# Copying the last 50 expert tiles' weights inside SBUF, gathering the third group without landing waits, two merged VectorE products, and new instruction orders

## What is computed

```python
x = x + ga * L0_attn(norm(x))            # RWKV: time mix, k, v, r, wkv scan, output, channel mix
x = x + gb * L0_ffn(norm(x))             # 128 -> 512 -> 128
x = x + ga1 * L1_attn(norm(x))           # softmax attention
h = norm(x); logits = h @ W_router + b_router
top_vals, top_idx = top_k(logits, 2)
for e in range(8):
    y = relu(h @ W1[e] + b1[e]) @ W2[e] + b2[e]      # 128 -> 512 -> 128
    out += y * softmax_weight[:, e]                  # 0 where e is not among the token's two
x = x + gb1 * out
```

## Time and profile before

| | before |
|---|---|
| median of 3 runs | 1623.48 us |
| lowest, highest | 1614.8, 1625.54 us |
| span of the profiled execution | 1622.0 us |
| PE busy | 1353.9 us (83%) |
| DVE busy | 1095.2 us (68%) |
| ACT busy | 990.8 us (61%) |
| POOL busy | 545.8 us (34%) |
| moved by DMA | 217.68 MB |
| loads of expert weights (mW, inner, wide) | 109 + 31 + 16, 514 KB each |

### The profile page before, as it was taken

One profiled execution on the slowest core, in us unless ns is written; L12 is line 12 of the kernel. 1 busy time (PEld: TensorE's weight loads), 2 busy tenths in 40 slices (PEclk: granted clock), 3 DMA queues, 4 the chain that ended last, 5 costly groups with the idle time before them and its releaser, 6 DMA issues.

```text
span 1622.0 us, 26719 instructions
## 1 busy us (share of the span) xinstructions
PE 1353.9 (83%) x8354; PEld 866.5 (53%) x8354; DVE 1095.2 (68%) x2943; ACT 990.8 (61%) x2295; POOL 545.8 (34%) x589
## 2 busy tenths in 40 slices
PE   3466897889888888999999979899899998998681
PEld 1234454534445444666666644467566754687571
DVE  5568879788989898676876895967755754140113
ACT  1354765667676556877777766567568565555430
POOL 2123222313122475212112256435322134344335
PEclk7677998989999889999999998799999999999885
DMA  4012135142321424454544524256555556788772
GB/s 126 7 36 72 42 114 167 46 132 64 110 77 30 121 83 116 139 157 124 168 134 141 154 87 137 78 164 193 159 169 171 159 166 207 225 275 276 225 244 76
DMA packets 202037, 217.68 MB, mean 134 GB/s; under 512 B 17419, under 2 KB 167526, under 8 KB 199593
## 3 DMA queue, kind: packets, MB, share of 16 engines
q1 hardware_dynamic: 193704, 199.18, 41.0%
q0 software_dynamic: 8192, 16.79, 3.4%
HBM read 161.18 MB, written 53.94 MB: 133 GB/s over the span
## 4 chain that ended last, share of the span: by engine, by line
PE 43%; DVE 21%; issue 11%; ACT 8%; POOL 7%; DMA 6%; SPq 2%; POOLq 0%; ACTq 0%; another core or an unknown queue 0%; DVEq 0%
DVE cmx L1581 6%; PE bank L1228 5%; PE bank L1045 5%; PE bank L1028 5%; PE bank L1212 5%; PE bank L1196 4%; PE bank L1151 3%; PE bank L1124 2%; POOL kg L775 2%; DMA kg<-y_slots,sslot 2%; PE bank L1164 2%; PE bank L1013 2%; POOL bhs L775 2%; ACT wide L903 2%; PE bank L1140 2%
## 5 line engine op out<-in xcount | busy, mean ns | idle before, releaser
L1581 DVE TENSOR_REDUCE cmx<-bank 128x2 f32<-128x512 f32 x512 | 328.7, 684 | 97.4 <-PE bank L1196 89.3
L903 ACT ACTIVATE wide<-bank 128x512 f32<-128x512 f32 x512 | 280.0, 609 | 69.2 <-PE bank L1212 64.6
L1212 PE MATMUL bank<-wide 75*128 75x512 bf16 x512 | 174.9, 407 | 23.2 <-DVE cmx L1581 14.7
L1196 PE MATMUL bank<-wide 72*128 72x256 bf16 x1024 | 176.2, 283 | 20.6 <-DVE cmx L1581 15.6
L756 POOL DMA_INDIRECT x_slots<-sx,sslot x128 | 128.1, 1001 | 111.3 <-issue 46.9
L1196 PEld LDWEIGHTS bank<-wide 72*128 72x128 bf16 x1024 | 92.0, 101 | 124.7 <-issue 48.2
L1228 PE MATMUL bank<-wide,bva 128*32 128x512 f32 x1024 | 146.5, 646 | 9.9 <-ACT wide L903 5.7
L942 ACT ACTIVATE mH<-bank,mW 128x128 f32<-128x128 f32 x376 | 107.0, 371 | 57.8 <-PE bank L1028 50.9
L1028 PE MATMUL bank<-mT,mW 128*128 128x128 f32 x872 | 123.8, 287 | 17.0 <-DMA mW<-in_wexp 7.9
L1028 PEld LDWEIGHTS bank<-mT,mW 128*128 128x128 f32 x872 | 112.6, 199 | 36.3 <-issue 14.7
L775 POOL DMA_INDIRECT kg<-y_slots,sslot x88 | 85.9, 976 | 117.9 <-DMA kg<-y_slots,sslot 35.6
(11 more groups left out here) (296 smaller groups left out, 2863.4 us busy)
## 6 DMA issues: line engine op xcount, KB each, us to landing
mW<-in_wexp SPq DMA_DIRECT2D x109, 514.0 KB
wide<-q_parts SPq DMA_DIRECT2D x32, 576.0 KB
inner<-in_wexp SPq DMA_DIRECT2D x31, 514.0 KB
wide<-in_wexp SPq DMA_DIRECT2D x16, 514.0 KB
mX<-x_slots SPq DMA_DIRECT2D x27, 256.0 KB
y_slots<-mX SPq DMA_DIRECT2D x27, 256.0 KB
q_parts<-bp SPq DMA_DIRECT2D x32, 192.0 KB
x_slots<-mH SPq DMA_DIRECT2D x2, 3072.0 KB, 10.9
```

What stands on the lines that cost most here:

```text
L903: act.activation(cP[:, i % 8, :], bank[seat["G_s", i]][:, :], ACT.Exp, scale=SCALE).then_inc(S["c_p"], 1)
L1196: ins = pe.matmul(ps[:, j * T:(j + 1) * T], cQ[0:SROWS, z, h, tt * P:(tt + 1) * P], cK[0:SROWS, z, h // G, :], start=True, stop=True)
L1212: pe.matmul(ps[:, :], cK[0:KROWS, z, g, sc_ * P:(sc_ + 1) * P], cQ[0:KROWS, z, h0:h0 + 2, :], start=True, stop=True).then_inc(S["c_s2"], 1)
L1581: dve.tensor_reduce(cmx[:, u % 2, tt, 2 * hp:2 * hp + 2], bank[seat["C_s", i]][:, :].rearrange("p (j t) -> p j t", j=2), AX_X, ALU.max, ne ...
```

## The change

1. WIDE goes: the last group has the same six places as the third. The tiles 106 to 155 (COPIED_TILE = LATE_TILE + 12) get their weights no more by loads from HBM. Instead SP loads all eight experts once into wide (M_e, eight loads of 514 KB), behind the last product that reads wide (c_pv), and DVE copies one expert's 1028 columns into the tile's place (M_c, 50 of them), with a register read from a new table seo (the column at which the expert starts).
2. The landing wait falls for the gathers of the third group too (WAITED_GROUPS = 2): K_g20 to K_g27.
3. In E_wkv2 two products of 512 columns become one of 1024; in G_o two of 64 become one of 128.
4. Words of the order tables of PE, ACT, DVE and SP are moved by a few places; on POOL 21 steps of 273, by one or two.

```diff
-INNER, WIDE = 4, 8
+WAITED_GROUPS = 2
+INNER = 4
+COPIED_TILE = LATE_TILE + 12
...
+        experts = wide[:, 0:EXPERTS * WROW]
         for t in range(MTILES):
             if t < LATE_TILE:
                 w_slots.append(t % 2)
-            elif t < FIRST_TILE[-1]:
+            else:
                 w_slots.append((2 + t - LATE_TILE) % (2 + INNER))
-            else:
-                w_slots.append((2 + INNER + t - FIRST_TILE[-1]) % SLOTS)
...
+                    if s == "M_e":
+                        if i == 0:
+                            sp.wait_ge(S["c_pv"], CHUNKS * BC * 4)
+                        sp.dma_start(experts[:, i * WROW:(i + 1) * WROW],
+                                     a["wexp"][i * P:(i + 1) * P, :]).then_inc(S["m_e"], 16)
...
-                        if GROUP_OF[c] < GROUPS - 1:
+                        if GROUP_OF[c] < WAITED_GROUPS:
                             landed(s, i)
...
-                        for j in range(2):
-                            v(dve.tensor_tensor(and_[:, j, :, :], aAB[:, j, :, 0:T], aP[:, 0, :, :], ALU.mult))
+                        v(dve.tensor_tensor(and_[:, :, :, :], aAB[:, :, :, 0:T],
+                                            aP[:, 0, :, :].unsqueeze(1).broadcast_to([P, 2, BC, T]), ALU.mult))
...
-                        for j in range(2):
-                            ins = dve.tensor_tensor(cctx[:, 2 * b:2 * b + 2, :, pp, j, :], t_[:, j, :, :, 0:HD],
-                                                    crs[:, 2 * j:2 * j + 2, :].unsqueeze(3)
-                                                    .broadcast_to([P, 2, KV, HD]), ALU.mult)
-                        ins.then_inc(S["c_ctx"], 1)
+                        dve.tensor_tensor(cctx[:, 2 * b:2 * b + 2, :, pp, :, :].rearrange("p t g j d -> p (t g) j d"),
+                                          CO[:, :].rearrange("p (j x v) -> p x j v", j=2, v=32)[:, :, :, 0:HD],
+                                          crs[:, :, :].rearrange("p (j t) g -> p (t g) j", j=2).unsqueeze(3)
+                                          .broadcast_to([P, 2 * KV, 2, HD]), ALU.mult).then_inc(S["c_ctx"], 1)
...
+                        dve.tensor_scalar(seo[:, i, 0:w_], sef[:, 0:w_], WROW / P, None, ALU.mult).then_inc(S["s_tile"], 1)
+
+                    if s == "M_c":
+                        t = COPIED_TILE + i
+                        g = place(t)[0]
+                        j = t - FIRST_TILE[g]
+                        k = w_slot(t)[0]
+                        if i == 0:
+                            dve.wait_ge(S["m_e"], 16 * EXPERTS)
+                        dve.wait_ge(S["s_tile"], 3 * (g + 1))
+                        dve.wait_ge(S["m_y"], w_before(t) + 1)
+                        at = dve.value_load(seo[0:1, g, j:j + 1], min_val=0, max_val=(EXPERTS - 1) * WROW)
+                        dve.tensor_copy(weights[k], experts[:, bass.ds(at, WROW)]).then_inc(S[f"m_w{k}"], 16)
...
+        G_o G_y M_c*2 R_ln K_sum K_out R_c M_c*3 R_lg R_m1 M_c*2 R_m2 R_e R_info S_cnt S_base M_c*2 S_slot
+        S_tile M_c*3 K_sum K_out M_c*18 K_sum K_out M_c*8 K_sum K_out M_c*4 K_sum K_out M_c*4 K_sum K_out M_c*4
+        K_sum K_out K_sum K_out K_sum K_out K_sum K_out
```

More of the change, by code:

```diff
@@ L91 @@
 s_zero s_tot s_pre s_base s_slot s_tile s_ldx0 s_ldx1 s_sc0 s_sc1
-m_ldx0 m_ldx1 m_ldx2 m_ldx3 m_ldx4 m_ldx5 m_st0 m_st1 m_st2 m_st3 m_st4 m_st5 m_w0 m_w1 m_w2 m_w3 m_w4 m_w5 m_w6 m_w7 m_w8 m_w9 m_w10 m_w11 m_w12 m_w13 m_tp m_x m_h m_r m_y m_o
+m_ldx0 m_ldx1 m_ldx2 m_ldx3 m_ldx4 m_ldx5 m_st0 m_st1 m_st2 m_st3 m_st4 m_st5 m_w0 m_w1 m_w2 m_w3 m_w4 m_w5 m_e m_tp m_x m_h m_r m_y m_o
 k_ld0 k_ld1 k_ld2 k_ld3 k_g0 k_g1 k_g2 k_g3 k_sum k_out k_st0 k_st1 k_st2 k_st3
@@ L330, in program @@
         sef = sb("sef", [P, SLOT_TILES])
-        sei = sb("sei", [P, GROUPS, SLOT_TILES], I32)
+        sei, seo = (sb(n, [P, GROUPS, SLOT_TILES], I32) for n in ("sei", "seo"))
         sx = sb("sx", [P, 2, NT, D])
@@ L339, in program @@
         weights += [inner[:, k * WROW:(k + 1) * WROW] for k in range(INNER)]
-        weights += [wide[:, k * WROW:(k + 1) * WROW] for k in range(WIDE)]
         quads = [mX[:, k, :, :] for k in range(MXS)] + [x_[:, :, :] for x_ in (az, ah, ez)]
@@ L1035, in mlp_out @@
                     if i == FIRST_TILE[g]:
-                        pe.wait_ge(S["s_tile"], 2 * (g + 1))
+                        pe.wait_ge(S["s_tile"], 3 * (g + 1))
                         if i == 0:
@@ L1745 @@
[L1745 to L1749, removed]
@@ L1760 @@
[L1760 to L1763, removed]
+        I_ld A_ld I_ldw I_ldx*16 I_st0 I_ldx*5 A_ldm I_ldx A_ldg I_ldx*7 I_st1 I_ldx*2 A_ld R_ldm I_ldx B_ldm
@@ L1764 @@
+        K_ldx M_st*2 M_ldx*2 K_st M_ldx M_st*3 K_ldx*3 M_ldx*2 K_ldx*2 K_st M_ldx K_ldx M_st K_st M_st*3 K_st
+        K_ldx M_st*2 K_st*4
         """,
@@ new lines @@
+        M_u E_n2 G_o B_w1 M_d E_xn2 A_n1 G_ct M_u A_xn M_d R_n E_fk M_t E_fk*3 R_h B_n1 B_h2 M_u E_fr R_e M_d
+        E_r M_u M_d C_mt M_u E_exp M_d G_s*2 B_split G_s*2 M_u G_s*3 B_split G_s*4 G_o G_s*2 A_n0 G_s M_d
+        B_split G_s*2 B_n0 B_h G_o B_w1 E_n2 B_w1*2 E_xn2 B_w1 C_mt A_n1 G_s*3 A_xn G_s*2 E_fk G_s*4 B_n1 G_s
+        G_o G_s*4 B_h2 G_s*2 E_fk*2 G_o E_fk E_fr G_ct E_r R_n C_mt E_exp B_split R_h G_s B_split G_s*5 M_t
+        B_split G_s M_u B_n0 G_s M_d A_n0 B_h M_u B_w1 G_o G_s*2 M_d G_s*2 M_u G_s*2 M_d G_s B_w1 G_s M_t B_w1
@@ L1830 @@
+        M_u*2 M_d*3 M_t M_u*2 M_d M_u*2 M_d*3 M_u*2 M_d M_t M_u*2 M_d*3 M_u M_d M_t M_u*2 M_d*2 M_u*3 M_d*3
+        M_u*2 M_d*2
         """,
@@ new lines @@
+        G_s*2 W_d*2 W_u*2 W_t G_o W_d*2 G_pv G_s G_pv W_u*2 W_d*2 W_u*2 W_d W_t G_o W_d G_ct W_u*3 G_wo W_d W_u
+        W_d W_t W_d*2 W_u*2 W_d W_u R_h R_lg W_u W_d*2 W_u W_t W_d S_pre W_d W_u*3 W_d*2 W_t W_u W_d*2 W_u*3
+        W_d*2 W_t W_d W_u*2 W_d W_u W_d W_u W_d*2 W_t W_u*2 W_d*2 W_u*2 W_t W_d W_u W_d W_u*2 W_d W_u W_d*2 W_t
+        W_u W_d W_u W_d W_u W_d*2 W_t W_u W_d W_u*3 W_d*2 W_t W_u W_d*2 W_u*2 W_d*2 W_t W_u*3 W_d W_u W_d*2 W_u
+        W_d W_t W_u W_d W_u*2 W_d*3 W_u W_t W_u W_d W_u*2 W_d*2 W_u*2 W_d*3 W_u*2 W_d*2
@@ L1941 @@
-        A_ln1s K_sum K_out E_ln2s R_info B_q*2 B_k G_o E_mix2 C_s*4 G_o B_v K_sum C_s K_out C_s G_y R_ln C_s*3
-        E_mix C_s*4 C_mp R_c E_out E_scan E_y B_ln0s C_s*6 E_wkv E_wkv1 K_sum K_out R_lg G_o R_m1 E_wkv2 E_rec
-        C_s E_att C_s*3 E_x1 C_s E_ln2s C_s*5 C_mp K_sum K_out C_s*5 G_o E_mix2 B_x2 B_ln1s R_m2 R_e G_o C_s
-        K_sum K_out C_s*7 B_q G_o C_s R_info C_s*2 E_out C_mp G_y R_ln B_q C_s*2 B_k C_s R_c B_v B_ln0s C_s*13
-        C_mp R_lg R_m1 G_o R_m2 R_e G_o R_info C_s*5 B_x2 G_o B_ln1s C_s*6 G_o C_s*5 C_mp G_y R_ln B_q C_s*3 B_q
@@ L1946 @@
-        R_c C_s*4 B_k C_s*8 B_v C_s C_mp R_lg R_m1 R_m2 R_e R_info S_cnt G_o S_base S_slot S_tile G_o C_s*7 G_o
-        C_s*9 C_mp G_o G_y R_ln C_s*9 R_c C_s*5 G_o C_s*2 C_mp R_lg R_m1 R_m2 R_e G_o*2 R_info K_sum K_out G_o
-        G_y R_ln K_sum K_out R_c R_lg R_m1 R_m2 R_e R_info S_cnt S_base S_slot S_tile K_sum K_out K_sum K_out
-        K_sum K_out K_sum K_out K_sum K_out K_sum K_out K_sum K_out K_sum K_out K_sum K_out
+        A_c E_rec E_att E_x1 E_ln2s A_ln1s B_x2 B_ln1s E_mix2 B_q*2 E_mix B_k E_out B_v E_scan E_y B_ln0s A_ln0s
@@ new lines @@
+        E_rec G_o R_m2 R_e C_s A_c C_s*9 G_o C_s*2 E_att C_s C_mp B_x2 B_ln1s E_x1 C_s*3 A_ln1s K_sum K_out
+        E_ln2s R_info B_q*2 B_k G_o E_mix2 C_s*4 G_o C_s*2 K_sum K_out C_s G_y R_ln B_v C_s*2 E_mix C_s*4 C_mp
+        R_c E_out E_scan E_y C_s*3 B_ln0s C_s*3 E_wkv E_wkv1 K_sum K_out R_lg G_o E_wkv2 E_rec E_att C_s R_m1
+        C_s*4 E_x1 C_s*2 E_ln2s C_s*3 C_mp K_sum K_out C_s G_o C_s*4 E_mix2 B_x2 B_ln1s R_m2 R_e G_o K_sum C_s*2
+        K_out C_s*4 B_q C_s G_o C_s*4 C_mp E_out G_y R_ln C_s*2 B_q R_info B_k C_s R_c B_ln0s C_s*4 B_v C_s*9
@@ new lines @@
+        C_mp R_lg R_m1 R_m2 G_o R_e G_o C_s*4 G_o B_x2 C_s*2 B_ln1s C_s R_info C_s*4 G_o C_s*5 C_mp G_y R_ln B_q
+        C_s*4 B_q R_c C_s*3 B_k C_s*9 C_mp B_v R_lg R_m1 R_m2 R_e R_info S_cnt S_base S_slot G_o*2 S_tile C_s*7
+        G_o C_s*9 C_mp G_o G_y R_ln C_s*6 R_c C_s*8 G_o C_s*2 C_mp R_lg R_m1 R_m2 R_e G_o*2 R_info K_sum K_out
+        G_o G_y M_c*2 R_ln K_sum K_out R_c M_c*3 R_lg R_m1 M_c*2 R_m2 R_e R_info S_cnt S_base M_c*2 S_slot
+        S_tile M_c*3 K_sum K_out M_c*18 K_sum K_out M_c*8 K_sum K_out M_c*4 K_sum K_out M_c*4 K_sum K_out M_c*4
```

346 lines of the change are left out of this document (166 added, 180 removed).

## The result

The changed kernel took 1646.63 us (median of 4 runs, 1640.09 to 1651.42) against 1624.51 for the kernel before in the same session: a ratio of 1.0164 (95% interval 1.0132 to 1.0196), slower by 1.6%. The forecast was 1594. The profiled execution took 1640.09, its span is 1638.3 us.

The account below looks back on a forecast made before the run. Bound in the tail by two chains ending within 4 us of each other, POOL's indirect transfers and PE's tiles. 1622.0 + 12 - 8 - 10.5 - 23.5 + 1.5 - 1.5 = 1592, median 1594 us; range 1575 to 1617.

Parts of the forecast that it names:

- Moved words: Order tables before 1385 us: steps move by one place on average, priced at 0 with 12 us either way.
- rival E: The moved words lose 12 us or more in the first 1385 us, total 1608 to 1620; chance 9%.
- K_g16 to K_g20: Tail, K_g16 to K_g19 on POOL: 43.7 us before, 33 forecast, a gain of 10.5 us.
- The flood: Eight expert loads after the last product reading wide delay K_st5's store and so K_g12: +9 us, bounds +1.5 and +14.
- The slots: Last group's slots on DVE, delayed by later sums and four showing copies: S_sc28 starts at 1461, +12 us.
- Scatters: Four scatter steps in the tail: 36.2 us before, 28.4 forecast with landings of 2.3 us, a gain of 8.
- rival A: The landings of scatters and gathers stay long, so the terms -8 and -10.5 go: 1612 us; chance 13%.
- TensorE's chain: PE's tail: S_pre3 at 1450.6, then 45 tiles at 2.5 us, ending at 1563, 1566 with the last store.
- rivals C and D: C: PE's last tiles are not held by weights, 1635, 6%. D: DVE becomes the bound, 1620, 6%.
- Rival B: DVE's 50 copies stop POOL from 1421 to 1564 us: 1629, or 1656 at 1.23 us a copy; chance 6%.
- Merged products: DVE products merged, 16 and 64 times, save some 5 us of DVE's time: 1.5 us gained, bounds 0 and 5.
- Taking away POOL's waits alone would gain next to nothing: Tail: POOL's and PE's chains end within 4 us of each other, so removing POOL's waits alone gains next to nothing.

Follow-up runs that it names:

- e1: The kernel before with only the moved words of all five engines up to the end of the attention: 1671.52 us, ratio 1.0325.
- e2: The changed kernel with the old step orders up to the end of the attention: 1590.57 us, ratio 0.9817 to the kernel before.
- e11: The kernel before with the changed orders of TensorE, VectorE and ScalarE only at about 545 to 605 us: 1632.76 us, ratio 1.0088.
- e4: The kernel before with the two merged VectorE products and nothing else: 1620.94 us, ratio 0.9999.
- e8: The kernel before without the landing waits of the third group's gathers, nothing else: 1608.26 us, ratio 0.9936.
- e9: The kernel before with all five engines' changed orders only up to about 650 us of the span: 1640.51 us, ratio 1.0113.

## Why the prediction was wrong, point by point

- **Moved words: the step that failed.** The forecast said "the steps move by one place on average", "0, with 12 either way", and rival E gave "12 us or more, 1608 to 1620" 9%. The runs show +50 (e1) to +56 (changed less e2) in its place. The average displacement says nothing of the cost; the 12 was a guess without a row under it, and one stretch of 60 us costs as much by itself (e11).
- **The tail: its gain right in sum, in part by luck.** Forecast 1594 with the front at nothing; e2, which is that kernel, took 1590.57. But the forecast has 190 us from the last product reading wide to the end (its sum of 1592 and the 1.5 of the merged products, less 1403.45), and measured are 195.8 (changed) and 198.9 (e2): 6 to 9 us more. The total hits because the terms were laid on one execution of before whose front ended at 1403.45, where e2's ends at 1389.99. In the terms, the slots came 4 us earlier than forecast, the scatters and K_g16 to K_g20 took 4 and 5 us longer.
- **The flood:** forecast K_g12 13 us behind the end of that product (1416.5 less 1403.45), measured 14.1 (1456.60 less 1442.5). Right. The store was issued behind six loads. The weights of the tile behind all eight took 10.29 us from their issue to their landing, in the chain that ended last; TensorE itself stood idle 0.92 us for them:

```profile
1450.15 10.29 DMA mW<-in_wexp
```

- **The slots:** S_sc28 was released by the CAST of sslot, as forecast, 53.6 us behind the product; forecast 57.5. The term of four copies at 1.5 us (6 us) was too large: a copy with its register read is 0.82 us where three stand in a row (starts at 1497.47, 1498.30 and 1499.1), not 0.69 and 0.85. From R_c15 to the slots are 21.4 us (19.4 before, 25.4 forecast).
- **Scatters:** 32.8 us, forecast 28.4, before 36.2. The scatters' landings came down to waits of 2.06 to 2.87, so rival A is out here; what is missing is in issues stretched beside other work, and one gap of 2.02.
- **K_g16 to K_g20:** 38.2, forecast 33. The step "Who waits for these copies' own waits is nobody" is wrong. Each copy waits for TensorE to leave its place, and VectorE's sums stand behind the copies. The two groups by line and shape:

```profile
L1731 DVE COPY inner<-wide 128x1028 f32 x34 | 25.1, 738 | 29.0 <-PE bank L1050 20.0 <-issue 6.8 <-DVE spos L1690 0.7
L1731 DVE COPY mW<-wide 128x1028 f32 x16 | 11.6, 724 | 15.8 <-PE bank L1050 12.6 <-issue 1.9 <-DVE rlg L1644 0.7
```

  Ahead of the sum that frees K_g18, VectorE does one copy per tile, three of them each after 2 us of waiting for L1050, and POOL waits 10.81 us at 1551.50. And one landing of a gather was long, with the weights' loads gone:

```profile
1561.62 0.94 POOL L780 DMA_INDIRECT kg<-y_slots,sslot  x1 [5.06 <-DMA kg<-y_slots,sslot]
```

- **K_g20 to K_g28:** 42.9, forecast 42. **K_g28 to the end:** 28.3, forecast 28.1.
- **TensorE's chain:** S_pre3 47.4 us behind the product (forecast 47.2), then 2.60 us a tile for 45 tiles (forecast 2.5), at a granted clock of 1.00 from 1496 to 1607. It waited for VectorE's copies 1.4 us in all. So rivals C and D are out.
- **The copy itself:** forecast 0.69 us, most say 0.70. Right.
- **Rival B (the copies stop POOL):** from 1456 on, 30 issues overlap with a copy and took 0.94 to 1.54 us, 1.15 on average; 66 do not, and half of them took 0.95 or less, the longest 1.21. That is some 6 us of POOL's time for 50 copies, 0.12 each, against the 0.59 from which B decides. By the rule cited ahead (the Trainium skill, "SBUF — State Buffer", "Who interferes with whom") a copy might have held POOL for its full 0.70; the trace shows interference of this kind, but of at most 0.6 us at one issue and none at others. It goes the other way too: the one copy of 1.68 us (at 1475.66) ran beside POOL's product rhn (at 1475.13, 1.66 us).
- **Merged products:** forecast 1.5 us gained, measured 0.2 within some 4 (e4: 0.9999), which cannot tell 1.5 from nothing. VectorE's busy time on these lines fell by 5.4 us, as computed: 1221 ns for two of 687, and 291 for two of 219 that overlapped:

```profile
L1488 DVE TENSOR_TENSOR inner<-inner 128x1024 f32<-128x1024 f32 x16 | 19.5, 1221 | 0.3
L1609 DVE TENSOR_TENSOR cctx<-bank,crs 128x128 f32<-128x128 f32 x64 | 18.6, 291 | 2.2
```

- **"Taking away POOL's waits alone would gain next to nothing":** wrong, 12 us (e8), through SyncE's list.

## What to carry to other kernels

An order written out by hand for several in-order engines is one object. A few places of difference on each cost 3% here, and TensorE's and ScalarE's tables alone 4.7%, and the mean displacement hides it: walk through the places where one engine's long operation covers another's short ones, and see whether the covered work still stands there and whether the bank that it needs is freed ahead. Put an order change and a data change into separate kernels, so that a gain of 30 us is not sold with a loss of 50. And two chains that share one in-order queue are not independent: look at what stands between their entries before calling one of them covered.

## What was not expected

- The cost of the orders by engine does not add (VectorE's 50, TensorE's with ScalarE's 76, all together 50), but that by stretch of time does (20 and 32). Within the front, most of what is lost in one place is not taken back: e9 is 18 us late at the 193rd mark and 20 at the last.
- Where TensorE waits, it also pays by its clock: in the window from 560 to 600 the granted clock was 0.79 against 0.88, and the product for B_q (two of 128x512) took 1.92 us at the lower of the two levels (0.50 from 592.9 to 594.9, behind a wait of 1.01 us) against 1.02 at the upper. In e11 that product takes 1.02 and the output product ahead of it 2.05 instead of 1.13, so the loss does not hang on the level at one product. What the clock's part of the 12 us is was not taken apart.
- 32 gathers of one transfer each 1.25 to 1.65 us after the other, none of them waiting for a landing, went through without any stall in the changed kernel, in e2 and in e8.
